# Turned totals in a PSUM bank of their own, half scores in two banks instead of three, rows finished three steps later

## What is computed

```
import jax, jax.numpy as jnp
# x: (8, 1024, 256); 16 heads of 16; window of 64 keys around a query
scores = einsum('bhqd,bhkd->bhqk', q, k) / sqrt(16)
scores = exp(scores - max(scores, axis=-1, keepdims=True))    # the maximum is over all 1024 keys
d = j - i
scores = where((d <= 31) & (d >= -32), scores, 0.0)
weights = softmax(scores, axis=-1)                            # of the masked values: those outside count as exp(0)
x = layernorm(x + (weights @ v) @ Wo)
# second stage: q, k, v = three trees (15 nodes, 16 leaves of 64); every row goes to one leaf of each tree
x = layernorm(x + softmax(q @ k.T / 16) @ v)
```

## Time and profile before

| | |
|---|---|
| median of 3 runs | 2,144.83 us |
| profiled execution | 2,150.88 us |
| its span | 2,148.9 us |
| mean granted TensorE clock of the span | 0.94 |
| busy over the span: PE, PEld, DVE, ACT, POOL | 1845.2, 1352.9, 1615.9, 1333.1, 897.3 us |
| maximum L1477, x1024 | 684.7 us busy, 681 ns each |
| matmul p_half L1036, x1024 | 402.9 us busy, 396 ns each |

### The profile page before, as it was taken

The page is one execution under the profiler, slowest core; times in us unless marked ns, Lnnn a source line. Parts: engine busy times, 40 slices in busy tenths (PEclk is TensorE's granted clock), DMA queues, the critical chain, the costliest instruction groups (busy, mean ns, idle before and its releaser), DMA issues. The chain is left out here.

```text
span 2148.9 us, 49579 instructions
## 1 busy us (share of the span) xinstructions
PE 1845.2 (86%) x16400; PEld 1352.9 (63%) x16400; DVE 1615.9 (75%) x4394; ACT 1333.1 (62%) x2515; POOL 897.3 (42%) x1338
## 2 busy tenths in 40 slices
PE   3988899889899898998988862877889599999997
PEld 2545556556455565564565551777778489999997
DVE  2887897977987978978978843796978367777775
ACT  2887787777787777777877722575766244444442
POOL 4422332554455456455545565000030755555511
PEclk8999999999999999999999965999999799999999
DMA  6443436336435535444454363969776333333311
GB/s 213 110 115 95 147 93 171 97 126 180 112 120 167 151 95 163 140 119 148 127 157 110 110 173 117 308 223 311 249 260 223 102 90 97 94 94 96 94 40 37
DMA packets 207318, 304.84 MB, mean 142 GB/s; under 512 B 48430, under 2 KB 108891, under 8 KB 207067
## 3 DMA queue, kind: packets, MB, share of 16 engines
q1 hardware_dynamic: 157322, 195.73, 31.1%
q0 software_dynamic: 29440, 68.98, 11.2%
q10 hardware_dynamic: 20304, 36.97, 4.7%
HBM read 104.16 MB, written 115.87 MB: 102 GB/s over the span
## 5 line engine op out<-in xcount | busy, mean ns | idle before, releaser
L1477 DVE CUSTOM_DVE_ANT_0 above<-p_half,above 128x512 f32<-128x512 f32 x1024 | 684.7, 681 | 99.2 <-ACT above L1156 66.9
L1156 ACT ACTIVATE above<-p_diff 128x512 f32<-128x512 f32 x1024 | 597.7, 605 | 224.1 <-PE p_diff L1032 213.3
L1036 PE MATMUL p_half<-k_stack,q_stack 96*128 96x512 bf16 x1024 | 402.9, 396 | 43.1 <-DVE row_max L1477 39.9
L1032 PE MATMUL p_diff<-d_stack,q_stack 96*128 96x512 bf16 x1024 | 406.3, 399 | 37.2 <-DMA d_stack<-d_parts 33.8
L1797 POOL DMA_INDIRECT raw<-sorted_y,slot x192 | 202.6, 1055 | 351.0 <-DMA sorted_y<-y_tile 295.9
L208 POOL DMA_INDIRECT sorted_x<-y,slot x192 | 198.6, 1034 | 92.7 <-issue 52.9
L2044 ACT ACTIVATE pt_hi<-p_one 128x512 fp32r<-128x512 f32 x128 | 69.5, 595 | 246.2 <-PE p_one L1920 246.2
L1036 PEld LDWEIGHTS p_half<-k_stack,q_stack 96*128 96x128 bf16 x1024 | 102.6, 101 | 139.7 <-DVE row_max L1477 117.7
L1177 ACT ACTIVATE w_win<-p_win 128x512 f32<-128x512 f32 x256 | 155.3, 607 | 47.7 <-PE p_win L1057 45.5
L1032 PEld LDWEIGHTS p_diff<-d_stack,q_stack 96*128 96x128 bf16 x1024 | 100.9, 99 | 127.3 <-issue 36.0
L1832 PE MATMUL p_out<-val_hi,pt_hi 128*128 128x256 f32 x512 | 151.8, 296 | 8.6 <-DVE val_lo L2113 7.9
(11 more groups left out here) (281 smaller groups left out, 4985.4 us busy)
## 6 DMA issues: line engine op xcount, KB each, us to landing
sorted_x<-zeros SPq DMA_DIRECT2D x141, 256.0 KB, 3.1
x_tile<-sorted_x SPq DMA_DIRECT2D x141, 256.0 KB, 4.1
sorted_y<-y_tile ACTq DMA_DIRECT2D x141, 256.0 KB, 3.6
q_stack<-q_parts SPq DMA_DIRECT2D x256, 96.0 KB, 2.4
k_stack<-k_parts SPq DMA_DIRECT2D x256, 96.0 KB, 2.4
d_stack<-d_parts SPq DMA_DIRECT2D x256, 48.0 KB, 2.0
v_win<-v_tiles POOLq DMA_DIRECT2D x16, 544.0 KB, 5.2
v_win<-v_tiles POOLq DMA_DIRECT2D x32, 272.0 KB, 6.0
```

Source lines behind the costliest of these rows:

```text
L1032: nc.tensor.matmul(p_diff[s % 2][:], qs, d_stack[0:SPLIT_ROWS, h, :], start=True, stop=True).then_inc(s_diff, 1)
L1036: nc.tensor.matmul(p_half[s % 3][:], qs, k_stack[0:SPLIT_ROWS, h, HALO + S // 2:HALO + S], start=True, stop=True).then_inc(s_half, 1)
L1156: nc.scalar.activation(above[:, s % 4], p_diff[s % 2][:], ACT.Relu).then_inc(s_above, 1)
L1477: nc.vector.tensor_tensor_reduce(out=above[:, s % 4], in0=p_half[s % 3][:], in1=above[:, s % 4], scale=1.0, scalar=-3.0e38, op0=ALU.add, o ...
```

## The change

- `p_half` gets two banks. The matmul of step k waits for the maximum of step k - 2, at every step (64 is a multiple of two).
- The freed bank is `p_turned`. The turn writes there; `inv` and `att` read there. In the last batch's tail two uses of the third half bank name `p_turned` instead.
- `weighted_values` of head k waits for the totals of head k - 1 (`s_tot`) instead of its finished rows (`s_att`).
- `ATT_LAG` goes from 39 to 42, so `inverse` and `attention` stand in step 2 of the following head instead of step 7. The turn stays at 39.
- `T0` and `T1` change places with `q1`: `q1` starts at step 32, `T0` at 36, `T1` at 40. In the last group `R2` takes the place before `T0` and `T1`.

```diff
-    0: [..., "S0", "q0", "T0", "T1", "q1", "k0", "k1", "d0", "K0", "X0", "X1"],
-    1: [..., "R0", "q0", "T0", "T1", "q1", "k0", "k1", "d0", "R1", "R2"],
+    0: [..., "S0", "q0", "q1", "T0", "T1", "k0", "k1", "d0", "K0", "X0", "X1"],
+    1: [..., "R0", "q0", "q1", "T0", "T1", "k0", "k1", "d0", "R1", "R2"],
...
-PV_LAG, TOTAL_LAG, TURN_LAG, ATT_LAG = 35, 36, 39, 39
+PV_LAG, TOTAL_LAG, TURN_LAG, ATT_LAG = 35, 36, 39, 42
...
-        p_half = [psum(f"p_half{i}", [P, 512]) for i in range(3)]
+        p_half = [psum(f"p_half{i}", [P, 512]) for i in range(2)]
...
-        p_turn = p_pv[:, 256:512].rearrange("p (n j e) -> p n j e", n=2, e=GROUP_ROWS)
+        p_turned = psum("p_turned", [P, 512])
+        p_turn = p_turned[:, 256:512].rearrange("p (n j e) -> p n j e", n=2, e=GROUP_ROWS)
...
-                    wait(pe, s_max, k + 1 - reuse(s, 3))
-                    nc.tensor.matmul(p_half[s % 3][:], qs,
+                    wait(pe, s_max, k + 1 - reuse(s, 2))
+                    nc.tensor.matmul(p_half[s % 2][:], qs,
...
                 pe.wait_ge(s_ww, k + 1)
-                wait(pe, s_att, k)
+                wait(pe, s_tot, k)
...
-                    ins = nc.tensor.transpose(p_pv[:, at:at + TURN_ROWS], total[0:TURN_ROWS, k % 2, P * n:P * n + P],
+                    ins = nc.tensor.transpose(p_turned[:, at:at + TURN_ROWS], total[0:TURN_ROWS, k % 2, P * n:P * n + P],
```

More of the change, by code:

```diff
@@ L55 @@
 JOBS = {
-    0: ["V0", "V1", "V2", "R3", "V3", "V4", "S0", "q0", "T0", "T1", "q1", "k0", "k1", "d0", "K0", "X0", "X1"],
-    1: ["O0", "O1", "O2", "O3", "X2", "X3", "R0", "q0", "T0", "T1", "q1", "k0", "k1", "d0", "R1", "R2"],
+    0: ["V0", "V1", "V2", "R3", "V3", "V4", "S0", "q0", "q1", "T0", "T1", "k0", "k1", "d0", "K0", "X0", "X1"],
+    1: ["O0", "O1", "O2", "O3", "X2", "X3", "R0", "q0", "q1", "T0", "T1", "k0", "k1", "d0", "R1", "R2"],
 }
@@ L63 @@
 LAST_JOBS = {
-    (B - 1, 1): (["O0", "O1", "O2", "O3", "R0", "R1", "T0", "T1", "R2", "R3"], [0, 4, 8, 12, 24, 28, 32, 36, 40, 44]),
+    (B - 1, 1): (["O0", "O1", "O2", "O3", "R0", "R1", "R2", "T0", "T1", "R3"], [0, 4, 8, 12, 24, 28, 32, 36, 40, 44]),
     (B, 0): (["K0"], [4]),
@@ L393, in window_attention @@
         bank_t = [p_half[0], p_half[1]]
-        bank_o = [p_diff[0], p_diff[1], p_half[2], p_job]
+        bank_o = [p_diff[0], p_diff[1], p_turned, p_job]
         bank_r = [p_half[0], p_half[1], p_diff[0], p_diff[1]]
-        bank_n = [p_win, p_half[2]]
+        bank_n = [p_win, p_turned]
         def four(t, i):
@@ L1477, in unit @@
                         nc.vector.tensor_tensor_reduce(
-                            out=above[:, s % 4], in0=p_half[s % 3][:], in1=above[:, s % 4], scale=1.0, scalar=-3.0e38,
+                            out=above[:, s % 4], in0=p_half[s % 2][:], in1=above[:, s % 4], scale=1.0, scalar=-3.0e38,
                             op0=ALU.add, op1=ALU.max, accum_out=row_max[g][:, s:s + 1]).then_inc(s_max, 1)
```

## The result

The changed kernel takes 2,201.45 us (median of 4 runs, 2,193.86 to 2,208.75), the kernel before 2,145.71 (4 runs). The ratio is 1.027, interval 1.0239 to 1.0301: 56 us slower. The forecast was 2,180 us, with a range from 2,140 to 2,222. The profiled executions, 48.6 us apart in span, show the place of the loss.

A forecast was written before the change was run, and what follows sets the result against it. No engine was full: TensorE, VectorE and ScalarE were coupled through a few PSUM banks. Two banks +54, T0 and T1 -15, group starts -5 gave +34 on 2,150.9, 2,185, less 6: 2,180 us, range 2,140 to 2,222.

The forecast's parts named there:

- head B: Profiled head in which VectorE is laden with jobs; its loop was put at 8.72 against 8.43 us, +0.29.
- over 350: Sign at p_half on TensorE: weight loads wait at 350 steps or more, with idle time at least twice 117.7 us.
- inside 25 to 55: Sign at the end of attention: the last maximum starts 25 to 55 us later than 1,235.7.
- +54: Cost of two p_half banks inside the heads: 0.45 us for 120 of the 128 heads, +54 us.
- - 15: Gain from moving T0 and T1 one place back: TensorE's wait for att before them goes, -15 us.
- - 5: Gain at group starts: p_half waits for one maximum earlier, about 0.7 us at each of seven starts, -5 us.
- The three heads: Three profiled heads, chosen for their differences, whose loops with two banks were worked out: mean +0.47 us a head.
- Head A: Profiled head where T0 and T1 leave TensorE little work; +0.60 to +1.06 us from its loop, taken as +0.8.
- C: Profiled head where VectorE waits 0.68 us for the turn; its loop was put at 9.93 against 9.61, +0.32.
- the loop I wrote down: Once a head: maximum 4, p_half 6, above 2, maximum 2, maximum 4; 8.72 to 9.93 us in three heads.
- VectorE's wait comes back: Faster rival: the 64.0 us wait for the turn vanishes and p_half's lateness is swallowed; 2,111 us, chance 0.16.
- Dearer: Rival: TensorE waits at p_half twice in every head, at steps 6 and 1; +82 us, 2,227 us, chance 0.14.

The follow-up runs named there:

- The own bank for itself: The changed kernel with inv and att back at step 39 and the old job order: 1.0484 of the kernel before, against 1.0496 without the turned totals' own bank.
- the rotation alone: The kernel before with its three p_half banks taken by the step's number in the whole run, not in its group of 64: ratio 0.9984.
- the order: The changed kernel with the p_half matmul of the next step issued at the end of TensorE's step instead of the front: 0.9988 of the kernel before.
- two banks alone: The kernel before with p_half in two banks instead of three and nothing else changed: ratio 1.0496.
- the two kernels: The changed kernel with inv and att at step 39 and the old job order, 1.0484 of the kernel before, and the changed kernel itself, 1.027.
- half of that work in front: The changed kernel with only job parts, transposes and node scores before p_half, 1.0186 of the kernel before, or only window scores, turn and weighted values, 1.0329.

## Why the prediction was right

**What was right, step by step.** The wait before `inv` fell to 2.7 us. The wait for `att` in front of T0 and T1, 15.1 us before, is in no row of the changed kernel. The own bank for itself shows no worth, as forecast. The release of p_half, 0.73 us from a maximum's start to the weight load, is 0.75 in head B. Weight loads wait at 565 steps (over 350), 2.7 times as long; VectorE waits more for `above`, at steps 7, 2 and 1 in 279 of 347 cases. The direction and its cause, a p_half that is refilled too late and holds up what stands behind it on in-order TensorE, are right. The last maximum starts 53.1 us later, inside 25 to 55. The rule that independent groups should rotate through different banks (the Trainium skill, Perfetto Trace Analysis, Matmuls) is kept in both kernels and doesn't decide: rotating two instead of three costs 5% alone.

**What was mis-sized.** The sum was +54 - 15 - 5 = +34, and the stretch from first to last maximum grew by 52.3. Measured on the trace, the 16 groups, each from its first to its last maximum, take 1,213.0 us instead of 1,147.0: +66.0. The 15 gaps between groups take 26.0 instead of 39.7: -13.7. So the total came nearer than its parts: the groups were forecast 27 us too low, the gaps 9 us too high, and that these partly cancel is luck.

- Inside the groups +54 - 15 = +39 was forecast. If the 15 us of T0 were really saved (the wait is gone; that it was time of the whole kernel no run shows), two banks and all that follows from them cost 81 us there, 0.63 a head and not 0.45 for 120 heads. This term, the +54, is the one that was mis-sized. The three heads say the same: +0.52, +0.55 and +0.91, mean 0.66. Head A was taken too high, B and C too low.
- B's working has a slip. It takes 0.05 us from the end of `above` to the maximum of step 2. A and C have 0.18 and 0.17, and B's own rows have 0.58 (730.57 - 729.99), for VectorE was busy then. With 0.17 B's loop gives +0.41 instead of +0.29.
- The rest was too low because the loop I wrote down runs once around the head, from step 4 over p_half of step 6 to step 2, and lets the head go on otherwise unhindered. p_half waits at 565 steps, not at one in a head, and the maximum of step 7, whose lateness I priced in head A only, waits in every one of the three heads (0.43, 0.37 and 0.29 us idle in the rows above) and in 110 of all 128. How it is held differs: by an exponential in front of `above` on ScalarE, which is a piece of the loop I wrote down, or by p_diff itself, which is the short loop. How much of the 81 us each of them costs stays open.
- The gaps had -5, for p_half's wait at a group's start. That wait is gone: 1.00 us at seven starts before, 0.12 us at each of them in the changed kernel. But it was almost hidden: where nothing else waits at such a start, the gap goes from 1.42 to 1.30 us (five of them), and with the rotation alone it stays at 1.42. So this term is worth under 1 us, not 5. What shortened the gaps is a wait that I didn't price: the load of the stack for the next group. In the kernel before, TensorE's wait for it was

```profile
PE p_diff L1032 <- DMA d_stack<-d_parts: 33.8, 9, 12.4
```

and it is 17.2 us in the changed kernel (12.4 of either at the very start). It stands at eight group starts before. The gaps of just these eight fall from 29.9 to 15.4 us, which is all of the -13.7 and a little more. Longer heads give the load more time, so a part of what a slower group costs comes back at its end.

**The rivals.** "VectorE's wait comes back" assumed that p_half's lateness is swallowed by waits already there. That did not happen: the wait before `inv` went from 64.0 to 2.7 us and the kernel is 56 us slower. Even where the order takes the loss away (0.9988) nothing of the 64 us shows as a gain. "Dearer" has near its size two banks alone (+106 us), but by another way, through the turn's wait of rows at 39. The share that moving the rows wins back, about 46 us by the two kernels, was never a term of the sum: I priced the final state only.

## What to carry to other kernels

How many buffers an in-order engine needs is not read from the buffer's own consumer alone, but also from what stands behind the waiting instruction. Before a bank is given away, compare the start of each refill with the release one buffer earlier; where it comes earlier, either keep the bank or put the refill behind all work that someone else waits for (here half of that work in front gave back 0.8% or nothing, all of it 2.8%). And a gain that is measured as idle time of one engine (64 us here) is worth only what the next wait behind it leaves.

## What the runs showed of the hardware

VectorE's release of a PSUM bank takes 0.69 to 0.76 us, median 0.75, from the start of a 128x512 maximum to TensorE's weight load, over the 559 loads of the changed kernel that had idled for the maximum two steps back. Two such maxima follow each other in 0.61 us (751.36 to 751.97 us in the trace before): the release comes after the next one may start.

The kernel before took 2,219 and 2,217 us on one chip, at a mean granted clock of 0.914 to 0.930, and 2,145 on another, at 0.937 to 0.946: 3.4% apart with the program unchanged. The second stage, which no edit touches, took 938 to 946 us in the traces of the first chip and 909 to 913 in the others. A difference of that size between chips is no result.
